# Two fused layers of an adaptive-layernorm model: four programs become two, landmark rows are stored ahead of the full rows, and the expert loop is unrolled with all its loads issued first

## What is computed

```python
mod = (_silu(L0_c) @ L0_wmod).reshape(8, 6, 1, -1)          # sa, ca, ga, sb, cb, gb; ga, gb kept away from 0
h = _layernorm(x) * (1 + ca) + sa
# layer 0 attention: 16 heads of 8 channels, 64 landmarks (means of 8 tokens)
L = softmax(q @ k_l.T); K = softmax(q_l @ k_l.T); N = softmax(q_l @ k.T)
for _ in range(6):                                          # V -> inverse of K
    KV = K @ V
    V = 0.25 * V @ (13 I - KV @ (15 I - KV @ (7 I - KV)))
x = x + ga * ((L @ (V @ (N @ v))) @ W_proj)
# layer 0 experts: 4096 tokens, top-1 of 8 experts, 512 slots each
x = x + gb * gathered(gelu(slots[e] @ w1[e]) @ w2[e])
# layer 1: attention with a bias that depends on the distance of two tokens
bias[h, d] = sum_k amp[h, k] * exp(-|sharp[h, k]| * (d - off[h, k]) ** 2)
# then a second attention (causal) and a top-2 mixture of 8 experts
```

## Time and profile before

| | us |
|---|---|
| median of three runs | 2140.73 |
| the profiled execution's own time | 2135.06 |
| its span (first to last instruction) | 2133.3 |
| PE busy | 1793.6 (84%) |
| DVE busy | 1463.0 (69%) |
| ACT busy | 1036.6 (49%) |
| POOL busy | 809.1 (38%) |
| share of the chain that ended last on PE | 39% |

### The profile page before, as it was taken

One profiled execution on the slowest core, in us unless ns is written; L12 is line 12 of the kernel. 1 busy time (PEld: TensorE's weight loads), 2 busy tenths in 40 slices (PEclk: granted clock), 3 DMA queues, 4 the chain that ended last, 5 costly groups with the idle time before them and its releaser, 6 DMA issues.

```text
span 2133.3 us, 56989 instructions
## 1 busy us (share of the span) xinstructions
PE 1793.6 (84%) x21312; PEld 1305.8 (61%) x21312; DVE 1463.0 (69%) x4552; ACT 1036.6 (49%) x2022; POOL 809.1 (38%) x1180
## 2 busy tenths in 40 slices
PE   3289898899963643999999999999999999999997
PEld 1167677777752422766666766766766766766665
DVE  6477778877760013777787787787787787778766
ACT  2045544555532211666655654554554555554542
POOL 0100101110011022766764664664664664664530
PEclk8589999999986866999999999999999999999999
DMA  4222222122006221102112112112112112111211
GB/s 144 67 90 69 65 56 59 43 73 57 7 8 208 69 64 61 60 10 76 56 42 83 54 41 83 55 41 83 54 41 82 55 41 81 51 43 43 86 31 46
DMA packets 89271, 132.19 MB, mean 62 GB/s; under 512 B 7834, under 2 KB 73754, under 8 KB 87339
## 3 DMA queue, kind: packets, MB, share of 16 engines
q1 hardware_dynamic: 54828, 98.31, 13.8%
q10 hardware_dynamic: 30848, 18.88, 3.0%
q0 software_dynamic: 3328, 11.40, 1.7%
HBM read 98.48 MB, written 30.23 MB: 60 GB/s over the span
## 4 chain that ended last, share of the span: by engine, by line
PE 39%; DVE 8%; DMA 7%; issue 5%; POOL 2%; ACT 2%; SPq 2%; ACTq 1%; POOLq 0%; DVEq 0%
PE ps L1592 12%; PE ps L1607 7%; PE ps L1578 5%; PE ps L1701 5%; PE ps L1687 4%; DMA l_stack<-parts_dram 3%; DMA l_w_e<-in_L_ffn_w_dram 2%; DVE l_X L1754 2%; PE ps L1638 1%; SPq L1382 1%; PE ps L1617 1%; POOL l_Y L1440 1%; ACT PT L1481 1%; DMA parts_dram<-l_parts 1%; DVE l_xn L1785 1%
## 5 line engine op out<-in xcount | busy, mean ns | idle before, releaser
L1440 POOL TENSOR_SCALAR l_Y<-l_X,l_nmax 128x512 f32<-128x512 f32 (+3 forms) x1024 | 674.4, 664 | 519.8 <-PE ps L1592 286.1
L1481 ACT ACTIVATE PT<-ps 128x512 f32<-128x512 f32 (+3 forms) x1024 | 519.8, 517 | 408.1 <-PE ps L1592 360.9
L1592 PE MATMUL ps<-ident,l_Y 128*128 128x128 f32 x3328 | 548.3, 279 | 13.6 <-ACT PT L1481 9.3
L1592 PEld LDWEIGHTS ps<-ident,l_Y 128*128 128x128 f32 x3328 | 386.4, 141 | 195.3 <-issue 82.3
L1754 DVE CUSTOM_DVE_ANT_0 l_X<-ps,strips 128x512 f32<-128x512 f32 x512 | 341.9, 687 | 135.2 <-PE ps L1578 132.0
L1578 PE MATMUL ps<-l_stack 72*128 72x512 bf16 (+3 forms) x1024 | 350.1, 344 | 68.5 <-DVE l_nmax L1754 50.4
L1754 DVE CUSTOM_DVE_ANT_0 l_X<-ps,mask 128x384 f32<-128x384 f32 (+3 forms) x512 | 238.5, 484 | 42.7 <-PE ps L1578 37.8
L1607 PE MATMUL ps<-PT,v_aug 128*10 128x128 f32 x6656 | 230.8, 274 | 0.0
L1607 PEld LDWEIGHTS ps<-PT,v_aug 128*10 128x10 f32 x6656 | 157.0, 91 | 71.3 <-ACT PT L1481 40.6
L1578 PEld LDWEIGHTS ps<-l_stack 72*128 72x128 bf16 x1024 | 101.9, 100 | 104.2 <-DVE l_nmax L1754 77.6
L1687 PE MATMUL ps<-l_fT,l_w_e 128*128 128x512 f32 x256 | 135.2, 616 | 12.3 <-DMA l_w_e<-in_L_ffn_w_dram 10.0
(11 more groups left out here) (280 smaller groups left out, 2593.8 us busy)
## 6 DMA issues: line engine op xcount, KB each, us to landing
stack<-parts_dram SPq DMA_DIRECT2D x48, 432.0 KB
l_stack<-parts_dram SPq DMA_DIRECT2D x64, 288.0 KB
l_stack<-parts_dram SPq DMA_DIRECT2D x192, 96.0 KB
l_w_e<-in_L_ffn_w_dram ACTq DMA_DIRECT2D x128, 128.0 KB, 2.3
parts_dram<-l_parts SPq DMA_DIRECT2D x32, 384.0 KB, 2.5
strips<-bias_dram POOLq DMA_DIRECT2D x16, 448.0 KB, 11.6
parts_dram<-parts SPq DMA_DIRECT2D x16, 432.0 KB, 2.6
w_e<-in_L_ffn_w_dram SPq DMA_DIRECT2D x16, 256.0 KB, 5.0
```

Source lines behind the costliest of these rows:

```text
L1440: nc.gpsimd.tensor_scalar(Y[:, n % Y_BUFS, 0:w], X[:, n % X_BUFS, 0:w], -1.0, nmax[:, n % 8:n % 8 + 1], ALU.mult, ALU.add).then_inc(y_pool, 1)
L1481: nc.scalar.activation(dst, src, ACT.Exp).then_inc(moved, 1)
L1592: last = nc.tensor.transpose(ps[:, to, k * P:(k + 1) * P], Y[:, n % Y_BUFS, k * P:(k + 1) * P], ident[:])
```

## The change

The four programs become two.

**Layer 0.** Setup and `nystrom_phase` become `layer0_phase`. x is loaded batch by batch (batch 0 by ACT's queue, batch 1 by SP, the rest later). The modulation rows are made on 8 partitions (one for each batch) for both layers at once; the gates are made on 8 x 256 elements, stored, and loaded back repeated. The bias table is made in eight pieces of 128 x 336: GpSimd does three operations, ScalarE the exponential, GpSimd one product, VectorE the sum, at steps -19 to 9 of the table (`GAUSS_AT`, `REDUCE_AT`). Landmarks leave `parts` and `stack` and get their own small tensors, `lm_parts` and `marks`; GpSimd makes their three parts (five operations); SP stores and loads them ahead of the full rows, and k's rows ahead of q's. For batch 0 the products from `Ks` to `a0` move from step -8 to step -28. Only `slots_in` is zeroed.

**Experts and layer 1.** `expert_programs` gives each engine's part without a loop, and `layer1_phase` runs it at its start, before its own instructions. All loads are issued at once (experts 0 and 1 weights by ACT, the rest by SP), each expert has its own buffer and semaphore, VectorE moves the transposed input out, SP stores, and the order on PE is hidden(e), turn(e+1), output(e-1). `strips` are loaded once expert 5's inputs are there. The first indirect load waits for the eight stores.

```diff
 FRONT, CORE = -2 * PHASES - 5, -PHASES + 10
+FIRST_CORE = FRONT + 13
+GAUSS_AT, REDUCE_AT, BIAS_AT, MODS_AT = -19, 2, PHASES + 2, -16
...
+                def store_marks(b):
+                    sp.wait_ge(lm_parts_ready, b + 1)
+                    if b:
+                        sp.wait_ge(marked, 64 * b)
+                    for s in range(2):
+                        sp.dma_start(marks_dram[s].rearrange("n p t -> p n t"), lm_parts[:, s]).then_inc(marks_stored, 16)
+                def mark(b):
+                    if b >= 2:
+                        wait_made(sp, ("L", b - 2, L_SIDES - 1))
+                    sp.wait_ge(marks_stored, 32 * (b + 1))
+                    sp.dma_start(marks[b % 2][:, 0].rearrange("r h t -> r (h t)"),
+                                 bass.AP(marks_dram.tensor, 0, [[0, 3], [H * NL, 3 * HD], [1, H * NL]])).then_inc(marked, 16)
+                    for i in range(3):
+                        thrice = bass.AP(marks_dram.tensor, (3 + i) * C * NL, [[0, 3], [H * NL, HD], [1, H * NL]])
...
+                for b in range(B):
+                    store_marks(b)
+                    mark(b)
+                    for s, stack_up in ((1, stack_k), (0, stack_q)):
+                        store(b, s)
+                        stack_up(b)
+                    if b == 0:
+                        sp.wait_ge(mods_ready, 1)
...
+                        for n in range(2, B):
+                            load_x(n)
+                        sp.wait_ge(mods_stored, 16)
+                        rows_of_0 = bass.AP(mods_dram.tensor, 0, [[0, P], [8 * C, B], [1, 3 * C]])
+                        sp.dma_start(mod_row0[:].rearrange("p b k c -> p b (k c)"), rows_of_0).then_inc(mod_rows_loaded, 16)
...
+                    if b == 1:
+                        for k in range(2):
+                            sp.wait_ge(bias_half_ready, k + 1)
+                            sp.dma_start(bias_dram[:, k * T:(k + 1) * T], bias_hr[:]).then_inc(bias_stored, 16)
...
+                def landmarks(b):
+                    for s in range(2):
+                        pool.wait_ge(lm_summed[s], b + 1)
+                    if b:
+                        pool.wait_ge(marks_stored, 32 * b)
+                    lm_chain.link(nc.gpsimd.tensor_scalar_mul(lm[:], lm[:], 1.0 / SEG))
...
+                def exponent(n):
+                    if n == 0:
+                        pool.wait_ge(shp_ready, 1)
+                    gauss_chain.link(nc.gpsimd.tensor_scalar(dist[:, n % 2], off_[:], rel[:, n:n + 1], None, ALU.subtract))
+                    gauss_chain.link(nc.gpsimd.tensor_tensor(gauss[:, n], dist[:, n % 2], shp[:], ALU.mult))
+                    nc.gpsimd.tensor_tensor(gauss[:, n], gauss[:, n], dist[:, n % 2], ALU.mult).then_inc(exponent_ready, 1)
...
+                def scaled(n):
+                    pool.wait_ge(gauss_ready, n + 1)
+                    nc.gpsimd.tensor_tensor(gauss[:, n], gauss[:, n], amp[:], ALU.mult).then_inc(gauss_scaled, 1)
...
+                columns(0)
+                pe.wait_ge(attn_loaded, 16)
+                pe.wait_ge(ny_loaded, 32)
+                pe.wait_ge(consts_pool, 12)
...
                     if name == "Ks":
-                        pe.wait_ge(stacked, 96 * (b + 1))
+                        pe.wait_ge(marked, 64 * (b + 1))
...
                 def statistics(n, b):
+                    if n == 0:
+                        dve.wait_ge(x_loaded[b], 16)
...
+    def sync_loads(sp):
+        for e in range(E):
+            sp.dma_start(x_e[:, e], slots_in[e * CAP:(e + 1) * CAP, :].rearrange("(t p) c -> p t c", p=P)).then_inc(expert_loaded[e], 16)
+            if e >= 2:
+                load_weights(sp, e)
...
+    def gpsimd(pool):
+        pool.wait_ge(expert_loaded[5], 48)
...
+        turn(0)
+        for e in range(E):
+            hidden(e)
+            if e + 1 < E:
+                turn(e + 1)
+            if e:
+                output(e - 1)
+        output(E - 1)
...
                 def gather(b, tiles):
                     if b:
                         pool.wait_ge(x_in, b)
+                    else:
+                        pool.wait_ge(experts_stored, 16 * E)
```

More of the change, by code:

```diff
@@ L494, in _ @@
+                sp.wait_ge(bias_stored, 32)
             @block.gpsimd
@@ new lines, in modulation @@
+                def modulation():
+                    dve.wait_ge(mods_made, 2)
+                    more = Chain(dve, mods_order).link
+                    for l in range(2):
+                        more(nc.vector.tensor_copy(mods[:, l].rearrange("b k c -> b (k c)"), ps[0:B, (1, NV_BANK)[l], :]))
+                    more(nc.vector.tensor_scalar_add(mods[:, :, 2, :], mods[:, :, 2, :], 1.0))
+                    for k in (0, 3):
+                        g = mods[:, :, k, :]
+                        more(nc.vector.tensor_scalar(sign[:], g, 0.0, 2.0, ALU.is_ge, ALU.mult))
+                        more(nc.vector.scalar_tensor_tensor(out=size[:], in0=g, scalar=-1.0, in1=g, op0=ALU.mult, op1=ALU.max))
+                        more(nc.vector.tensor_scalar_max(size[:], size[:], 0.25))
+                        more(nc.vector.tensor_scalar_sub(sign[:], sign[:], 1.0))
+                        last = nc.vector.tensor_tensor(g, sign[:], size[:], ALU.mult)
+                        if k == 0:
+                            more(last)
+                    last.then_inc(mods_ready, 1)
@@ new lines, in gpsimd, with scalar @@
+    def gpsimd(pool):
+        pool.wait_ge(expert_loaded[5], 48)
+        for h in range(H):
+            src = bass.AP(bias_dram.tensor, h * 2 * T, [[1, P], [1, STRIP]])
+            pool.dma_start(strips[:, h, :], src).then_inc(strips_loaded, 16)
+    def scalar(act):
+        for e in range(2):
+            load_weights(act, e)
+        for e in range(E):
+            if e >= 2:
+                act.wait_ge(ex_y_ready, e - 1)
+            for f in range(FT):
+                act.wait_ge(hidden_ready, e * FT + f + 1)
+                nc.scalar.activation(hid[:, e % 2, f, :], ps[:, 2 + f, :], ACT.Gelu_apprx_tanh).then_inc(hidden_evac, 1)
@@ new lines, in vector, with turned, output @@
+    def vector(dve):
+        def turned(e):
+            dve.wait_ge(ex_xT_ready, e + 1)
+            nc.vector.tensor_copy(xT_e[:, e % 2], ps[:, e % 2, :]).then_inc(ex_xT_evac, 1)
+        def output(e):
+            dve.wait_ge(ex_y_ready, e + 1)
+            nc.vector.tensor_copy(y_e[:, e], ps[:, 6 + e % 2, :].rearrange("p (t c) -> p t c", t=CT)).then_inc(ex_y_evac, 1)
+        turned(0)
+        for e in range(E):
+            if e + 1 < E:
+                turned(e + 1)
+            if e:
+                output(e - 1)
+        output(E - 1)
@@ L1242, in layer1_phase @@
         y0 = sb("y0", [P, TT, C])
+        v_aug = [sb(f"v_aug{a}", [P, TT, H, VW]) for a in range(2)]
+        gb0_now = sb("gb0_now", [P, C])
+        mid_rows = sb("mid_rows", [P, 3, C])
+        gb_now = sb("gb_now", [P, C])
+        experts_stored = sem("experts_stored")
+        strips_loaded = sem("strips_loaded")
+        experts = expert_programs(nc, sb_, sem, ps, ident, strips, bias_dram, slots_in, slots_out, experts_stored,
+                                  strips_loaded, ex_w1, ex_w2)
         stats = [sb(f"l1_stats{n}", [P, TT, 6]) for n in range(2)]
```

611 lines of the change are left out of this document (308 added, 303 removed).

## The result

| | before | after |
|---|---|---|
| median (us) | 2142.41 (4 runs, 2138.5 to 2160.65) | 2073.06 (4 runs, 2066.66 to 2078.45) |
| ratio | | 0.9645, 95% interval 0.9602 to 0.9688 |
| span of the profiled execution | 2133.3 | 2071.5 (its own time 2073.5) |
| busy TensorE, VectorE, GpSimd | | 1779.4, 1444.1, 857.9 |

What follows compares the result with a forecast made beforehand. Two empty stretches were taken to bound it: the wait for step 0 and the hole around the experts. 2135.06 - 47.1 + 0 - 52.2 = 2035.8 us profiled, plus 3 for the median: 2039 us, range 2018 to 2060.

Steps and rivals of the forecast that it cites:

- First transposes to `a0`: Start of layer 0: first transposes at 12 us, `Ks` at 31, `a0` at 43.1.
- The bias table on GpSimd: Ahead of step 0: eight pieces of 3.4 us, 28.7 us with landmarks; step 0 at 75.7 instead of 122.85 us.
- The rival with a quick GpSimd: Before step 0: two-input operations near 0.60 us, batch 2's x binds, step 0 at 70, total 2033 us; chance 0.15.
- SP now makes 14 DMAs a batch for 8, but all within about 40 us of a batch's 62: Layer 0's steady part: SP's added DMAs fit within a batch, adding no time.
- the rival on SP's chain: Layer 0: SP's serial stores, waits and loads make each batch 13 us longer, 104 in all, 2143 us; chance 0.02.
- The DMA path binds: Before step 0: loads behind k's stack at half rate, step 0 at about 90, total 2053 us; chance 0.12.
- The steady part: Layer 0's batches: VectorE loses about 0.8 us a batch, half counted over eight batches, -3 us.
- From step 0 to the next power: Layer 0 from step 0: eight bias sums in steps 2 to 9, +1 us; TensorE entering at clock 0.50, +2 us.
- Experts: Expert phase: 8.14 us an expert, first indirect load at 725.3 instead of 777.47 us, 52.2 us gained.
- The bound on feeding: Expert phase: three loads an expert take over 8.14 us, so PE waits; ten us lost give 2049 us; chance 0.08.
- The median: Whole kernel: the runs' median is 5.7 us above the profiled execution; 3 us of these added, giving 2039 us.

Runs made afterwards that it cites:

- run 1: Changed kernel with the two bias-table stores issued from GpSimd's queue instead of SP's: 2049.5 us, ratio 0.9533.
- run 5: Changed kernel with two buffers for the k and q parts (even and odd batches), SP's order untouched: 2050.2 us, ratio 0.9546.
- run 7: Changed kernel with four of the eight bias-table pieces issued from step -2 on instead of ahead of step 0: 2071.5 us, ratio 0.9641.
- run 2: Changed kernel with both stores of a batch (k and q) issued ahead of both stack loads: 2058.7 us, ratio 0.9574.
- run 12: Changed kernel with the 16 bias strip loads (7 MB) not waiting for the sixth expert's inputs: 2080.6 us, ratio 0.9669.
- run 4: Changed kernel with layer 1's second gate row loaded ahead of the first stack instead of behind it: 2052.1 us, ratio 0.9548.
- the tenth run: Changed kernel with the edits of run 1, run 2, run 4, run 5 and run 7, and batch 2's x loaded at SP's start: 2015.6 us, ratio 0.9377.

## Why the prediction was wrong

**First transposes to `a0`: right.** 10.7, 29.99 and 41.31 for 12, 31 and 43.1.

**The bias table on GpSimd: mechanism right, one term mis-sized.** I named the piece as what step 0 would wait for, and it was. The two-input operations took 0.89 us for my 0.85. The one-input one, a subtraction, took 1.12, where I had interpolated 0.60 between two rows of another operation, a multiplication with an addition; the bounds I gave were for the other three. Eight times 0.52 is 4.2 us, most of what the pieces took more. In all GpSimd needed 34.9 us from its first piece (43.55) to the power (78.42), where I had 28.7, and began 1.3 us earlier. Step 0 came at 81.1 for 75.7. The rival with a quick GpSimd fell with it. The estimate from the Trainium skill, "GPSIMD Engine Reference", section "Elementwise — side-by-side cycle accounting" (0.74 us for two inputs), is below the measured 0.89.

**"SP now makes 14 DMAs a batch for 8, but all within about 40 us of a batch's 62": this step failed, and it is 24 of the 34 us.** I counted SP's work per batch (a batch takes 64.7 us in the trace, not 62, which changes nothing here) and found room, and left out two things of its order. The stores of the bias table are in that order once, behind batch 1, and wait for step 20; all of batch 2 stands behind them. And I asked when landmarks and k must be *loaded*, 21 steps later, not when the parts must be *stored*: the consumer with the earliest need is VectorE's next split, through `parts`. In the rival on SP's chain I priced a steady 13 us a batch and gave it 0.02; what came was two waits of VectorE in one batch, 22.5 us together, which runs 1 and 5 remove by two different cures.

**"The DMA path binds" (0.12): priced too low, in the wrong place.** I had it 6 us ahead of GpSimd at step 0, and it was indeed covered there: VectorE took batch 2's x at 60.23 without a wait, for my 66. But it continues behind step 0: in run 7 the step moved 15 us and batch 1's stores did not, and the gain ended in a wait at 102 us. So, by run 7, the 5.4 us by which step 0 came late hardly count at the end of this kernel.

**The steady part: -3 forecast, +4 measured.** From the power of batch 0's second norm to that of batch 7's (214.79 to 623.64, and 205.20 to 617.99) the changed kernel takes 412.8 us for 408.9. VectorE does have less work (52.08 for 52.44 us in a batch of 65), but such a batch is 0.35 us longer, not shorter: work taken off an engine with 12 us of idle time a batch gained nothing. That is 1.4 us over the four batches from 205 to 465 us; the rest stands behind them. Runs 1, 2 and 5 show the same 413 to 414 us. What adds it I did not test.

**From step 0 to the next power: +1 for bias sums and +2 for the clock forecast, +5.9 measured.** Eight sums at 0.49 us stand here, four of them between 95 and 105 us, where VectorE is busy 4.9 of 5 us, and this stretch took 43.9 to 49.7 us in runs of nearly the same program, so that some of it is scatter. It stays open how it divides.

**Experts: right, 3.4 us better.** 647.79 is 12.6 us behind the last scatter's issue (11.7 forecast). From there to the last output moved are 65.3 us for 70.0. I summed the durations of transposes, hidden and output, 8.14 us an expert. Here they take 0.60, 3.60 and 3.74 us, and each group starts some 0.16 us before the record of the one ahead of it ends, so an expert takes 7.45. The bound on feeding was not reached, and run 12 shows how near it is.

**The median** of the kernel before lies 7 us above its profiled execution in these four runs, that of the changed one 0.4 us below its own; so the medians are 69 us apart where the spans are 62, and of the miss of 37.5 us in the spans only 34 us are seen between forecast and median.

## What to carry to other kernels

When a queue's program order gets a wait added, list everything behind it and ask for each store when its *source* buffer is written again: that need comes earlier than the load's deadline, and it is found by searching the waits on the store's semaphore. A count of work per period says nothing of a one-off wait in it. And an earlier start is only worth what the next queue lets through: of 15 us, 1.6 were left here until a second buffer let 17 through.

## What I had not expected of the hardware

A store of 384 KB issued on the queue behind three loads that keep few engines busy took 16.4 us, where k's took 4.8, and a row of 512 bytes behind such loads 14.9 us: on one queue the small transfer pays for the loads ahead of it, and runs 2 and 4 took 14.3 and 20.9 us off by issuing it ahead of them. From 175 to 185 us these loads moved 86 GB/s at a DMA share of 0.20, so 80% of the engines' time was idle while the store waited.

On GpSimd, subtracting a column held in one value per partition (one input of 128 x 336) took 1.12 us, more than the product of two inputs of the same size (0.89), and more than layer 1's multiplication and addition with such a value on 128 x 512 (0.76). The modulation on 8 partitions, 13 small operations, took 10.6 us of VectorE, twice what I had put down. Operations on the same 8 x 256 elements differ:

```profile
46.80 0.65 DVE L995 SCALAR_TENSOR_TENSOR size<-mods 8x256 f32<-8x256 f32 x1
47.48 0.42 DVE L996 TENSOR_SCALAR size<-size 8x256 f32<-8x256 f32 x1
47.94 0.94 DVE L997 TENSOR_SCALAR sign<-sign 8x256 f32<-8x256 f32 x1
48.91 1.07 DVE L998 TENSOR_TENSOR mods<-sign,size 8x256 f32<-8x256 f32 x1
```

These four take the same again at their second turn and in the tenth run. That does not make it a property of the operation, since in each of these places the same work of GpSimd runs beside them. At 47.85 and at 48.81 GpSimd starts products of 0.89 us each; the operations of 0.94 and 1.07 us start 0.1 us behind them and end 0.1 to 0.3 us behind their ends, and a subtraction of two inputs on 128 x 512 elements took only 0.69 us (at 55.65). So it looks as if VectorE was held until GpSimd's product was through. No run has these operations without GpSimd beside them, so this is not shown. It cost nothing at step 0 here, since GpSimd's chain was longer.

TensorE's granted clock fell to 0.74 and 0.66 in the hole from 160 to 200 us: VectorE's waits there sum to 22.5 us and the stretch was 26.3 us longer than before (76.5 for 50.2 us from batch 3's power on). Between the same two powers TensorE's 851 matmuls were busy 54.5 us at a mean granted clock of 0.84, and 50.0 us at 1.00 in run 1, whose stretch took 52.9 us. How much of these 4.5 us reached the end is not shown: the two stretches differ by 23.6 us, 1.1 more than the waits.
